# The second cross attention of a two-layer transformer kernel: values ahead of the query projection on TensorE

## The reference

```python
def attention(q_in, kv_in, wq, wk, wv, wo, bo):
    b, n, _ = q_in.shape
    l = kv_in.shape[1]
    q = (q_in @ wq).reshape(b, n, H, HD).transpose(0, 2, 1, 3)
    k = (kv_in @ wk).reshape(b, l, H, HD).transpose(0, 2, 1, 3)
    v = (kv_in @ wv).reshape(b, l, H, HD).transpose(0, 2, 1, 3)
    scores = jnp.einsum('bhnd,bhld->bhnl', q, k) * HD ** (-0.5)
    probs = jax.nn.softmax(scores, axis=-1)
    out = jnp.einsum('bhnl,bhld->bhnd', probs, v)
    return out.transpose(0, 2, 1, 3).reshape(b, n, H * HD) @ wo + bo
...
h = layer_norm(hidden_states, norm2_g, norm2_b)
hidden_states = attention(h, encoder_hidden_states, attn2_wq, attn2_wk, attn2_wv, attn2_wo, attn2_bo) + hidden_states
```

## Time and profile before

| | us |
|---|---|
| time, median of 3 runs | 4255.37 |
| lowest and highest run | 4243.68, 4258.28 |
| time of the profiled execution | 4251.52 |
| its span, first to last instruction | 4249.7 |
| loop of slots 3 to 61 of the changed stage | about 3513.5 to 3905 |

### The profile page before, as it was taken

The page is one execution under the profiler, slowest core; times in us unless marked ns, Lnnn a source line. Parts: engine busy times, 40 slices in busy tenths (PEclk is TensorE's granted clock), DMA queues, the critical chain, the costliest instruction groups (busy, mean ns, idle before and its releaser), DMA issues. The chain is left out here.

```text
span 4249.7 us, 64423 instructions
## 1 busy us (share of the span) xinstructions
PE 3913.7 (92%) x24639; PEld 2600.7 (61%) x24639; DVE 2773.3 (65%) x4577; ACT 1839.0 (43%) x2746; POOL 1791.5 (42%) x1155
## 2 busy tenths in 40 slices
PE   0799999996897997998999999999999979999899
PEld 0633434433456886885666666666666647777787
DVE  6489999982445655445667676766767637665565
ACT  0437777773443233442333333333333324444332
POOL 0269830001112102003777877877787753222200
PEclk9869999997789998997999999999999989999999
DMA  4655334313631104884121111112111010000100
GB/s 124 206 69 74 56 52 48 37 19 63 105 55 49 25 13 147 304 309 148 51 76 51 51 70 56 51 51 75 51 51 69 33 31 10 10 10 1 39 14 20
DMA packets 314598, 294.30 MB, mean 69 GB/s; under 512 B 133277, under 2 KB 237789, under 8 KB 314037
## 3 DMA queue, kind: packets, MB, share of 16 engines
q1 hardware_dynamic: 312052, 282.53, 25.9%
q0 software_dynamic: 2240, 7.66, 0.6%
HBM read 161.26 MB, written 127.28 MB: 68 GB/s over the span
## 5 line engine op out<-in xcount | busy, mean ns | idle before, releaser
L1729 POOL TENSOR_TENSOR f_sums<-f_sums,f_probs 128x1024 f32<-128x1024 f32 x384 | 915.4, 2384 | 154.4 <-ACT f_probs L1848 117.2
L1848 ACT ACTIVATE f_probs<-f_st 128x1024 f32<-128x1024 f32 x512 | 525.0, 1027 | 939.4 <-PE f_st L1894 934.6
L1746 DVE TENSOR_REDUCE f_mx<-f_s 128x1 f32<-128x512 f32 x1024 | 659.8, 686 | 381.3 <-PE f_s L1871 369.9
L1358 DVE TENSOR_REDUCE f_mx<-f_s 128x1 f32<-128x512 f32 x1024 | 638.6, 683 | 51.4 <-PE f_s L1489 29.4
L1469 ACT ACTIVATE f_probs<-f_st 128x512 f32<-128x512 f32 x1024 | 536.0, 601 | 203.9 <-PE f_st L1506 203.6
L1871 PE MATMUL f_s<-f_k,f_q 64*128 64x512 f32 x3072 | 515.0, 415 | 18.5 <-DMA f_k<-k 12.3
L1894 PE MATMUL f_st<-f_q,f_k 64*128 64x512 f32 x3072 | 485.4, 390 | 1.1 <-ACT f_probs L1848 1.0
L1908 PE MATMUL f_acc<-f_probs,f_v 128*64 128x512 f32 x2048 | 465.2, 596 | 0.0
L1871 PEld LDWEIGHTS f_s<-f_k,f_q 64*128 64x128 f32 x3072 | 341.5, 189 | 166.3 <-issue 112.0
L1894 PEld LDWEIGHTS f_st<-f_q,f_k 64*128 64x128 f32 x3072 | 367.0, 184 | 25.4 <-ACT f_probs L1848 3.6
L1506 PE MATMUL f_st<-f_q,f_k 50*128 50x512 f32 x1024 | 334.3, 476 | 7.2 <-ACT f_probs L1469 6.6
(11 more groups left out here) (316 smaller groups left out, 7958.9 us busy)
## 6 DMA issues: line engine op xcount, KB each, us to landing
q<-f_stage SPq DMA_DIRECT2D x80, 512.0 KB, 2.8
k<-f_stage SPq DMA_DIRECT2D x80, 512.0 KB, 2.8
f_q<-q SPq DMA_DIRECT2D x32, 1024.0 KB, 5.0
f_k<-k SPq DMA_DIRECT2D x32, 1024.0 KB, 7.3
v<-f_v_stage SPq DMA_DIRECT2D x64, 256.0 KB, 3.1
f_v<-v SPq DMA_DIRECT2D x32, 512.0 KB, 8.5
f_q<-q SPq DMA_DIRECT2D x96, 128.0 KB, 4.3
f_k<-k SPq DMA_DIRECT2D x96, 128.0 KB, 7.0
```

The costliest lines, as they stand in the source:

```text
L1358: v.tensor_reduce(mx[:, i % 2, c:c + 1], bank[u % 4][:, :], AX_X, ALU.max).then_inc(s_free, 1)
L1729: g_.tensor_tensor(out, out, probs[:, n % NP, :, :], ALU.add).then_inc(sum_done, 1)
L1746: v.tensor_reduce(mx[:, i % 2, c:c + 1], bank[u % 3][:, :], AX_X, ALU.max).then_inc(s_free, 1)
L1848: a_.activation(probs[:, s % NP, :, :], stb[s % 2][:, :, :], ACT.Exp, scale=L.scale).then_inc(p_ready, 1)
```

## The change

On PE, in every iteration, `values(n - 3)` now stands directly behind `score(n)` and `query` behind both. ScalarE and VectorE take the two results in the same new order (output parts first, then query parts), and the list of PSUM banks is filled in the new order. Nothing else is changed: the same instructions with the same operands. It touches the 59 iterations that have both, n = 3 to 61.

```diff
         for n in range(FIRST, LAST):
+            if acc_of(n - 3):
+                unit("acc", *acc_of(n - 3))
             for key in q_of(n):
                 unit("q", *key)
-            if acc_of(n - 3):
-                unit("acc", *acc_of(n - 3))
...
                     if y_of(n - 1):
                         project(*y_of(n - 1))
+                    if acc_of(n - 3) and not narrow:
+                        low_out(*acc_of(n - 3))
                     for key in q_of(n):
                         low_query(*key)
-                    if acc_of(n - 3) and not narrow:
-                        low_out(*acc_of(n - 3))
...
+                    if acc_of(n - 3):
+                        high_out(*acc_of(n - 3))
                     for key in q_of(n):
                         high_query(*key)
-                    if acc_of(n - 3):
-                        high_out(*acc_of(n - 3))
                     if turn_of(n - 2):
                         scale(turn_of(n - 2))
...
                     if 0 <= n < SLOTS:
                         score(n)
+                    if acc_of(n - 3):
+                        values(n - 3)
                     for key in q_of(n):
                         query(*key)
-                    if acc_of(n - 3):
-                        values(n - 3)
                     if y_of(n):
                         project(*y_of(n))
```

## The result

The changed kernel takes 4268.31 us (median of 10 runs, 4260.21 to 4288.29) against 4252.39 us of the kernel before (10 runs, 4241.43 to 4258.99). The ratio is 1.0046 with a 95% interval from 1.0031 to 1.0060: 0.46% slower, and the interval leaves out no change. Its slowest run lies 28 us above its fastest; the ten runs of the kernel before spread over 17.6 us.

A forecast was written before the change was run, and what follows sets the result against it. PE was taken to bound the stage; 4.6 us from pauses less saved surcharges plus 13.6 from clock falls made 18.2 us slower, 4269.7 us profiled or 4273.6 against the median, range 4256 to 4288.

The forecast's parts named there:

- The neighbours on PE: Reordered matmul kinds on PE: fewer surcharges between neighbours, saving 0.15 us per plain slot and 0.20 per slot with a project.
- The two pauses: At values, places 3 and 7 of six tiles: PE waits 0.93 and 2.15 us for ScalarE's late copy.
- the margin of 0.2 us: Ordinary slots: the copy ends 0.2 to 0.3 us before PE wants it, so these slots don't wait.
- rival C: Ordinary slots: the margin fails, 41 slots wait 0.2 to 0.4 us each, 4290 us or more; chance 0.07.
- The sum without the clock: Whole stage: 7.1 us lost in six tiles less 2.5 gained in slots 48 to 61, 4.6 us slower.
- Rival A: The pauses come but PE's clock stays up: 4.6 us slower, 4260.0; chance 0.27 with up to four falls.
- The first tile: The tile of the first slots, without project at 3 and 4 and with other waits: counted as the others, within 1 us.
- The clock: PE's clock falls behind five of six long and three of six short pauses: 8 x 1.7 = 13.6 us slower.

The follow-up runs named there:

- e4_filler: The changed kernel with matmuls of no use in the pauses at places 3 and 7 of six tiles; 4251.61 us against 4253.33 before, ratio 1.0007.
- e5_stats0: The changed kernel with the norm's statistics made at place 0 instead of place 1; 4264.11 us against 4252.70 before, ratio 1.0031.
- e3_only3: The kernel before with the new order only at place 3 of six tiles; 4255.94 us, ratio 1.0013.
- e2_only7: The kernel before with the new order only at place 7 of six tiles; 4264.23 us against 4253.33 before, ratio 1.0035.

## Why the prediction was right, and where a size was off

**Direction, size and mechanism held.** Forecast 18.2 us slower; the ratio gives 0.0046 x 4252 = 19.6 us, the medians 15.9. The predicted 4273.6 us is 5.3 above the measured median, 3 of which are the shown median of before against that of the ten runs.

**The neighbours on PE.** The plain slot was forecast at 4.94 us and is 4.94. Score to values was to cost what score to query did: 1.47 us at 3602.01. The slot with a project was to save 0.20. The one that the forecast was read from saves 0.30: before, it goes from 3679.36 to 3687.33, 7.97 us, and after the change such slots take 7.67. The 24 steps of its project now take 3608.72 - 3605.99 = 2.73 us, 0.114 each, where I had taken 0.118 from the earlier trace rows. But that slot stands for 16 of the 28 only; in the other 12 the project's steps were as short before, as at n = 56 (3874.04 - 3866.16 = 7.88 us), and these save 0.21. Rows of the kernel before:

```profile
3679.36 0.30 PE L3008 MATMUL f_s<-f_k_hi,f_q_hi 64*128 64x78 f32 x2
...
3866.16 0.31 PE L3008 MATMUL f_s<-f_k_hi,f_q_hi 64*128 64x78 f32 x2
...
3874.04 0.30 PE L3008 MATMUL f_s<-f_k_hi,f_q_hi 64*128 64x78 f32 x2
```

The term was undersized by some 0.10 x 16 = 1.6 us. Why the project's steps were slower in some slots before stays open.

**The two pauses.** Forecast 0.93 and 2.15 us, measured 0.85 to 0.86 and 2.08 to 2.09 from the second tile on, five times each. Both chains, VectorE's statistics and ScalarE's scaling, kept their length, and in those tiles nothing else waited. The ordinary slots don't wait, as the margin of 0.2 us said (rival C is out). In the first tile the waits are 1.07, 0.87 (at place 6, behind a wait of PE for the turn of the norm; I had not counted this one, and its cause stays open) and 1.60.

**The sum without the clock.** 4.6 us forecast, 3.0 with the project's term corrected. From the second tile on the corrected forecast is 5 x 1.18 - 2.5 - 1.6 = 1.8 us, and 1.5 is what the changed kernel shows there without its falls, 1.7 the kernel with fillers, which has none. Rival A (the pauses without the clock, 4.6 us) is what e4_filler comes to, 3 us by the ratio.

**The first tile.** "I count it as the others, within 1 us" is the step that failed. It is 9.7 us longer in the profiled execution, where the forecast gives a tile 1.2 without the clock and some 2.3 for its share of the falls. Two of its three falls are behind the pauses at places 3 and 7; the third, at place 6, begins before the wait for the copy there, where the kernel before has its only fall too, and lasts 6.8 us instead of 3.4. Even with the pauses filled this tile is 3.8 us longer. This is where the stage's 4.9 us above the forecast sum come from: the 54 iterations behind it are 13.4 us longer, where 3.4 + 11.3 = 14.7 were forecast for them.

**The clock.** This is the term on which the case turned: 13.6 us forecast, from eight falls of 1.7. The profiled execution has eight behind pauses, four behind the six long ones (I had taken five) and four behind the six short ones (three). That the number came out is partly luck: e5_stats0 has the same pauses of 2.08 us and had five falls in five. A fall of 3.4 us costs 1.5 to 1.6 us, close to the 1.7, but four of the nine falls of the stage last 3.4 or 3.5 us and five 6.8 or 6.9, 48.0 us in all and 44.4 more than before.

For many runs this can be estimated, since each timed run has its mean granted clock. The ten runs of the changed kernel have 0.9455 on average, 35 and 26 runs of the kernel before 0.9484 and 0.9490. With the two levels 1.00 and 0.50 that is 465 us at the low clock in the whole program against 438 and 434, so 27 to 32 us more and at most 13 to 16 us of time. The forecast's 13.6 was of the right size. The profiled execution fits this: 454 us in all against 429 in that of before, 44 more in the changed stage and 19 less elsewhere. Within the changed kernel's ten runs time and low clock go together (correlation 0.97). That its runs spread more widely than those of before is not shown: the 35 runs of before reach from 4236 to 4271 us.

The Trainium skill (TensorE: Matmul & The Clock Gate, HAM oscillation) warns of pauses longer than any here. The trace disagrees: pauses of 0.9 and 2.1 us in dense work were followed by the low clock in eight cases of twelve, and filling them ended it.

## What to carry to other kernels

When a matmul group is moved ahead of the one that covered its operand's latency, look for the places in the loop where the producer is late for another reason (here a norm step every eighth slot): the ordinary slot says nothing of them. On TensorE a pause should be priced twice, by itself and by the clock; here the second was the larger (from the second tile on 11.9 us in six falls, against 1.5 for pauses and neighbours together), and matmuls of no use in the pause, or the old order at the two late places only, took it away. An order that is better in most slots and bad in a few is worth splitting by place: that gained 0.2 to 0.3% where the uniform change lost 0.46%.

## What the runs showed of the hardware

A pause of 0.85 us in an otherwise dense stretch of TensorE was followed by a fall of the granted clock from 1.00 to 0.50 in three of five cases of the changed kernel, one of 2.08 us in three of five as well (the first tile's, 1.07 and 1.60 us, both had one). With the same pauses of 2.08 us e5_stats0 had five falls in five, and with pauses of 0.55 us e3_only3 had one in five. The short one at place 3 of the second tile of the changed kernel, and the window behind it:

```profile
3565.00:3568.00 3.00, 2.14 (x9) 1.07 (x8) 2.97 (x5) 1.50 (x2) 2.53 (x8) 0.87 0.00 0
3567.20:3570.60 3.40, 3.40 (x12) 2.84 (x12) 2.01 (x5) 1.80 (x3) 1.92 (x5) 0.50 0.00 0
```

PE was busy 2.14 of 3 us around it, and then 3.4 us without a gap at 0.50. Yet 2.08 us of pause up to 3595.81 left the clock at 1.00 (first fence of the section on the result, windows from 3593.60 on), so length alone does not decide. A fall of 3.4 us made a slot 1.5 to 1.7 us longer, one of 6.8 us 2.7 to 3.2 (changed kernel, e2_only7, e5_stats0).

The two tiled kinds of matmul stand behind each other for the price of one change: score to query, 1.46 us start to start, is the same as score to values, and query to project lost the surcharge of 0.10 us that values to project had.
